# The PV matmuls of two attention units put behind one another, and one exponential moved a quarter back

## The chip, the cores and the metric
The kernel runs on one core of a Trainium2 chip. The metric is the device time of one execution in microseconds. Before the change the median of three runs is 512.85 us (512.27 to 514.27).

## The reference
A block of a conditioned transformer on 32 sequences of 128 tokens, with 128 features, 16 heads of 8 features, and a hidden width of 512. Cut to what matters:

```python
x = rmsnorm(tokens, attn_norm_w)
scale, shift = jnp.split(modulation @ film_w.T + film_b, 2, axis=-1)
x = x * (1.0 + 0.1 * jnp.tanh(scale))[:, None, :] + shift[:, None, :]
q, k, v = jnp.split(x @ qkv_w.T + qkv_b, 3, axis=-1)          # q and k then get RoPE
tokens = tokens + merge_heads(masked_attn(q, k, v, valid)) @ out_w.T + out_b
query, src = rmsnorm(tokens, sq_norm_w), rmsnorm(seq_tokens, s_norm_w)
update = merge_heads(masked_attn(query @ wq.T, src @ wk.T, src @ wv.T, svalid)) @ mha_out_w.T  # + biases
gate = jax.nn.sigmoid(jnp.concatenate([tokens, update], axis=-1) @ gate_w.T + gate_b)
tokens = tokens + gate * update
g, val = jnp.split(rmsnorm(tokens, ffn_norm_w) @ gu_w.T + gu_b, 2, axis=-1)
return tokens + jax.nn.silu(g) * val @ down_w.T + down_b

def masked_attn(q, k, v, valid_keys):
    scores = jnp.einsum('bhqd,bhkd->bhqk', q, k) / math.sqrt(HD)
    scores = jnp.where(valid_keys[:, None, None, :], scores, jnp.finfo(scores.dtype).min)
    return jnp.einsum('bhqk,bhkd->bhqd', jax.nn.softmax(scores, axis=-1), v)
```

## The kernel before
The 32 sequences are eight groups of four. Each group has a self and a cross attention, so there are 16 phases. A phase has four units, one per sequence, with all 16 heads: 64 units. Two units are a pair (32 pairs), and a pair's results leave PSUM together.

All engines run the same loop over time steps t. `n, q = divmod(t, 4)` gives a unit n and a quarter q, four heads. What an engine does in a step is written into its loop by hand, in a fixed order; it runs its list in order and is held only by semaphores. In the steps of unit n:

- TensorE makes the scores from which the maxima of unit n + 4 are taken (`max_scores`, line 366, into the two banks `ps_a` by turns), and the transposed scores of unit n (`prob_scores`, line 386, into the two banks `ps_b` by turns). q and k are split in three bf16 parts each and stacked, so both are bf16 matmuls. The scores of quarter q wait until the bank's user of two quarters ago is done.
- VectorE takes the maxima (`maxima`, line 1087) and splits them in two bf16 parts (`split_tops`). TensorE turns them (`turn_tops`, line 374), ScalarE copies them (`keep_top`, line 888), and ScalarE's DMA queue writes them as two more rows of the stacked q (`top_rows`, line 895). The scores of line 386 thus have the maxima subtracted. The first quarter of an even unit waits for that DMA (`top_in`).
- ScalarE takes the exponential of each quarter (`exps`, line 902) into `probs`, which holds an even and an odd unit. The first exponential of unit n waits until the PV matmuls of unit n - 2 are done.
- TensorE multiplies the probabilities with the values (`weigh`, line 403): per unit 16 fp32 matmuls, 32 columns of the array each, which the trace shows as 32. They write one half of the bank `ps_o`, the even unit the left, the odd one the right. The padded values hold a column of ones, so the sum of the exponentials comes along. `weigh(n - 1)` stands ahead of everything else in quarter 2 of unit n.
- VectorE takes the pair (`take_pair`, lines 1105 and 1107: transpose of `ps_o`, reciprocal of the sums) in quarter 3 of the even unit behind it, and divides it (`divide_pair`, lines 1117 and 1125) in quarter 1 of the odd one.

The other products stand between these at steps of their own: projections and value products of later groups (lines 320, 331, 353), the two output projections (`out_product` of line 415, "mo" of line 320), norms (`column_means` of line 425, for which ScalarE squares in line 931; `turn_factors` of line 433), the gate (439, 440) and the hidden layer (320, 444, 455, 461). They use three banks `ps_g` by turns, and the score banks once these are free at the end. A phase's first scores wait for the stacks of q and k (line 658, SyncE's DMA queue) and its mask row.

Of the kernel before, what the change touches and what calls it, by code (L numbers as in the profile page):

```python
# [37 lines left out]
UNITS = PHASES * NG  # L38
PAIRS = UNITS // 2
# [70 lines left out]
def build(nc, x, side, cond, mask, anw, qkv_w, qkv_b, out_w, out_b, film_w, film_b, sqw, snw, in_w, in_b,  # L110
          mo_w, mo_b, gate_w, gate_b, fnw, gu_w, gu_b, down_w, down_b, cos_t, sin_t, ident_t, out):
    with ExitStack() as ctx:
# [189 lines left out]
        def _(pe):  # L302
# [87 lines left out]
            def weigh(n):  # L390
                p, b = divmod(n, NG)
                u = n % 2
                if b == 0:
                    taken(pe, ("v", p))
                if u == 0:
                    wait(pe, o_taken, n // 2)
                pe.wait_ge(exp_done, NQ * (n + 1))
                for r in range(2):
                    for j in range(2):
                        for c in range(4):  # L400
                            h = 4 * c + 2 * r + j
                            at = 26 * h - 8 * j
                            mm = pe.matmul(  # L403
                                ps_o[32 * c:32 * c + 32, u * 256:(u + 1) * 256].rearrange(
                                    "p (b r q) -> p r b q", r=2, q=32)[:, r],
                                v_pad[p % 2][:, b, at:at + 32],
                                probs[:, u, h * S:(h + 1) * S].rearrange("k (b q) -> k b q", q=32),
                                start=(j == 0), stop=(j == 1))
                mm.then_inc(pv_done, 1)
# [82 lines left out]

            for t in range(FIRST, LAST):
                n, q = divmod(t, 4)
                if q == 2 and 0 <= n - 1 < UNITS:
                    weigh(n - 1)
                if n + LEAD == 0 and q == 0:
                    pe.wait_ge(ones_in, 16 * 2 * SETS)
# [309 lines left out]
        def _(act):  # L808
# [153 lines left out]
            for t in range(FIRST, LAST):  # L962
                n, q = divmod(t, 4)
                for m in range(PAIRS):
                    if t == top_time(m) + 1:
                        keep_top(m)
                if 0 <= n < UNITS:
                    exps(n, q)
                for m in range(PAIRS):
                    if t == top_time(m) + 1:  # L970
                        top_rows(m)
                for g in range(G):
                    sp_at, cp_at = POS[SELF, g], POS[CROSS, g]
                    for b in range(NG):
                        if g and t == s_prep(g) - 16 + x_square_at(g)[b]:
                            square(SELF, g, b)
                        if t == ck_prep(g) - 16 + (5, 6, 7, 8)[b]:
                            square(CROSS, g, b)
                        if t == s_prep(g) + 2 + b // 2:
                            keep_xm(g, b)  # L980
                    if t == s_prep(g) + 10:
                        act.wait_ge(summed[0], g + 1)
                        keep_hi(0, sp_at)
                    if t == s_prep(g) + 12:
                        act.wait_ge(summed[1], g + 1)
                        keep_hi(1, sp_at)
                    if t == s_prep(g) + 13:
                        keep_mid(0, sp_at)
                    if t == s_prep(g) + 14:
                        keep_mid(1, sp_at)  # L990
                    if t == c_prep(g) - 3:
                        residual1(g)
                    if t == c_prep(g) - 2:
                        square2(g)
                    if t == ck_prep(g) + 1:
                        keep_side(g)
                    if t == ck_prep(g) + 5:
                        keep_full(("ck", g), 1, C_CKB, cp_at)
                    if t == ck_prep(g) + 6:
                        taken(act, ("ck", g))  # L1000
                        keep_hi(1, cp_at)
                    if t == cq_prep(g) + 9:
                        keep_full(("cq", g), 0, C_CQB, cp_at)
                    if t == ck_prep(g) + 9:
                        keep_mid(1, cp_at)
                    if t == cq_prep(g) + 10:
                        taken(act, ("cq", g))
                        keep_hi(0, cp_at)
                    if t == cq_prep(g) + 13:
                        keep_mid(0, cp_at)  # L1010
                    if t == post(g, "tanh"):
                        gate(g)
                    if t == post(g, "square"):
                        square3(g)
                    for j in range(4):
                        if t == mlp(g)[0][j] + 1:
                            gated_unit(g, j)
                if t == s_prep(0) + 8:
                    keep_weights(2, four(ps_a[0])[:, 0:2, :], W_V, W_V + 2)
                    keep_late_weights("cv_weights", W_CV, W_CV + 1)  # L1020
                for o in (1, 2):
                    for p in range(2):
                        if t == s_prep(p) + (0, 14, 16)[o]:
                            stack_k(o, p)
                for k in range(4):
                    if t == (0, 3, 5, 8)[k] + 1:
                        keep_late_weights(("weights", k), (W_MO, W_GU, W_GU + 4, W_DOWN)[k],
                                          (W_MO + 3, W_GU + 4, W_GU + 8, W_DOWN + 4)[k])
                if t == 10:
                    src = full_in(act, "late")  # L1030
                    act.activation(late[:, 0:N_L], src[:, 0:N_L], ACT.Copy).then_inc(taken_sem("late"), 1)
                    taken(act, "late")
                if t == 16:
                    act.wait_ge(halves_set, 2)

        @block.vector
        def _(dve):
# [198 lines left out]
            for t in range(FIRST, LAST):  # L1236
                n, q = divmod(t, 4)
                if n % 2 == 0 and q == 0 and 0 <= (n + 2) // 2 < PAIRS:
                    split_tops((n + 2) // 2)
                if 0 <= n + LEAD < UNITS:  # L1240
                    maxima(n + LEAD, q)
                if n % 2 == 0 and q == 3 and 0 <= (n - 2) // 2 < PAIRS:
                    take_pair((n - 2) // 2)
                if n % 2 == 1 and q == 1 and 0 <= (n - 3) // 2 < PAIRS:
                    divide_pair((n - 3) // 2)
                for p in range(PHASES):
                    if t == v_time(p) + 1:
                        keep_v(p)
                for g in range(G):
                    if g and t == s_prep(g) - 16 + (14 if g < 4 else 11):  # L1250
                        means_x(g)
                    if t == ck_prep(g) - 16 + 9:
                        means_side(g)
                    if 0 < g < 4 and t == s_prep(g):
                        norm_x(g)
                    for r in range(2):
                        for which in range(2):
                            if t == s_prep(g) + 6 + 2 * r + (which if g >= 4 else 0):
                                rope(r, g, which)
                    if t == c_prep(g):  # L1260
                        mean_of(("ss2", g), ms2)
                    if t == c_prep(g) + 4:
                        normed2(g)
                    if t == post(g, "update"):
                        update(g)
                    if g >= 5 and t == post(g, "residual"):
                        residual2(g)
                    if t == post(g, "mean"):
                        mean_of(("ss3", g), ms3)
                    if t == post(g, "normed"):  # L1270
                        normed3(g)
                    for j in range(4):
                        if t == mlp(g)[2][j]:
                            hidden(g, j)
                    if t == mlp(g)[3][1] + 1:
                        add_down_bias(g)
                if t == s_prep(0) + 10:
                    order_heads(2, ps_a[0][:, 2 * D:4 * D], W_CQ)
                    dve.wait_ge(v_bias_in, 32)
                if t == 12:  # L1280
                    taken(dve, "late")
                    dve.tensor_scalar(half_gate_b[:, :], late[:, L_GB:L_GB + 1], 0.5, None, ALU.mult
                                      ).then_inc(halves_set, 1)
                    dve.tensor_scalar(half_g_b[:, :], late[:, L_GUB:L_GUB + 4], 0.5, None, ALU.mult
                                      ).then_inc(halves_set, 1)
# [45 lines left out]
```

## Time and profile before

| | |
|---|---|
| runs: median (lowest to highest) | 512.85 us (512.27 to 514.27) |
| profiled execution | 517.94 us, of which the span is 516.1 |
| mean granted TensorE clock | 0.937 of full speed |
| TensorE matmul / weight load busy | 442.1 us (86%) / 308.3 us (60%) |
| VectorE busy | 350.1 us (68%) |
| ScalarE busy | 290.4 us (56%) |
| GpSimd busy | 190.8 us (37%) |
| line 403 (PV), matmuls / weight loads | 73.3 us / 55.3 us, 2048 each |
| line 366 and line 386 (scores), matmuls | 105.0 us and 102.0 us, 1024 each |
| line 1087 (maxima) | 169.6 us, 256 of 680 ns |
| line 902 (exponentials) | 151.3 us, 256 of 595 ns |

The profiled execution is one of its own, with its own time beside its span. Busy shares are means over stages with different limits. A matmul's end is modelled, so a start minus the start before it says more than its length. "Idle before" a row is the engine's own idle time, with what released it.

### The profile page before, as it was taken

The numbers are of one execution on the slowest core, as the hardware profiler recorded it, in microseconds if no ns is written. First come the engines' busy times: TensorE is split into PE (matmuls) and PEld (weight loads), VectorE is DVE, ScalarE is ACT, GpSimd is POOL, SyncE is SP. The second block draws the span as 40 slices with busy tenths as digits, with TensorE's granted clock in tenths as the row PEclk, the third lists the DMA queues.
The fourth block names the chain that finished last, engine by engine and source line by source line (L and its number), as shares of the span: only waits on it lengthen the run. The fifth ranks groups of instructions, "written<-read, shape, count | busy, mean of one in ns | idle before, by whom it ended". The sixth has DMA issues, their size and how long they took to land.

```text
span 516.1 us, 13226 instructions
## 1 busy us (share of the span) xinstructions
PE 442.1 (86%) x5219; PEld 308.3 (60%) x5219; DVE 350.1 (68%) x655; ACT 290.4 (56%) x644; POOL 190.8 (37%) x184
## 2 busy tenths in 40 slices
PE   3546889878897986999989988999999969999897
PEld 2115375756675664666577655866586748565664
DVE  2326655878885896698677866767748856856565
ACT  4321364577566664777576648486636744556243
POOL 4451140614433163528381828254542542000010
PEclk9975778899997999799999999999989999999999
DMA  3355442354353445344443443425140320000001
GB/s 77 87 174 174 131 122 88 100 162 151 100 162 107 140 121 153 103 128 121 131 137 108 117 140 97 153 67 163 43 149 25 98 92 3 23 3 22 22 1 42
DMA packets 62942, 52.04 MB, mean 101 GB/s; under 512 B 3803, under 2 KB 61728, under 8 KB 62880
## 3 DMA queue, kind: packets, MB, share of 16 engines
q1 hardware_dynamic: 60050, 49.07, 32.2%
q10 hardware_dynamic: 2830, 2.12, 1.4%
q8 instruction: 42, 0.69, 0.6%
q14 instruction: 20, 0.16, 0.1%
HBM read 8.55 MB, written 2.11 MB: 21 GB/s over the span
## 4 chain that ended last, share of the span: by engine, by line
PE 52%; DVE 11%; DMA 10%; ACT 8%; issue 8%; SPq 5%; POOL 4%; ACTq 1%; DVEq 0%; POOLq 0%
PE ps_o L403 8%; PE ps_a L366 7%; PE ps_g L320 7%; PE ps_b L386 6%; PE ps_g L461 5%; SPq L658 4%; DMA k_st<-part_k 4%; DVE top L1087 4%; PE ps_g L444 4%; PE ps_g L353 3%; DMA q_st<-top_t 3%; ACT probs L902 2%; DMA s_in<-in_fside_BxSxS 1%; ACT turned_in L838 1%; PE ps_g L418 1%
## 5 line engine op out<-in xcount | busy, mean ns | idle before, releaser
L1087 DVE TENSOR_REDUCE top<-ps_a 128x4 f32<-128x512 f32 x256 | 169.6, 680 | 106.1 <-PE ps_a L366 104.8
L902 ACT ACTIVATE probs<-ps_b 128x512 f32<-128x512 f32 x256 | 151.3, 595 | 143.6 <-PE ps_b L386 139.5
L366 PE MATMUL ps_a<-k_st,q_st 73*128 73x128 bf16 x1024 | 105.0, 228 | 27.8 <-DMA k_st<-part_k 15.0
L366 PEld LDWEIGHTS ps_a<-k_st,q_st 73*128 73x128 bf16 x1024 | 69.8, 101 | 79.5 <-issue 59.9
L386 PE MATMUL ps_b<-q_st,k_st 75*128 75x128 bf16 x1024 | 102.0, 223 | 9.4 <-ACT probs L902 7.5
L386 PEld LDWEIGHTS ps_b<-q_st,k_st 75*128 75x128 bf16 x1024 | 69.6, 99 | 18.5 <-issue 9.2
L403 PE MATMUL ps_o<-probs,v_pad 128*32 128x128 f32 x2048 | 73.3, 287 | 0.0
L403 PEld LDWEIGHTS ps_o<-probs,v_pad 128*32 128x32 f32 x2048 | 55.3, 115 | 24.1 <-issue 14.7
L728 POOL TENSOR_TENSOR f<-f 128x4 f32<-128x4 f32 x16 | 16.6, 1038 | 98.8 <-DVE f L1136 98.8
L320 PE MATMUL ps_g<-norm,w_t 128*128 128x512 f32 x66 | 37.1, 647 | 1.2 <-DVE hid L1178 1.2
L320 PE MATMUL ps_g<-turned_in,w_t 128*128 128x512 f32 x48 | 30.3, 717 | 5.0 <-ACT turned_in L838 4.8
L444 PE MATMUL ps_g<-norm,w_t 128*128 128x512 f32 x56 | 30.1, 620 | 3.3 <-DVE quotient L1132 2.6
L461 PE MATMUL ps_g<-w_t,hid 128*128 128x128 f32 x224 | 27.4, 276 | 0.0
L765 POOL TENSOR_SCALAR unit_th<-unit_th 128x512 f32<-128x512 f32 x16 | 9.9, 620 | 45.0 <-ACT unit_th L922 45.0
L461 PEld LDWEIGHTS ps_g<-w_t,hid 128*128 128x128 f32 x224 | 26.0, 192 | 0.0
L922 ACT ACTIVATE unit_th<-ps_g,half_g_b 128x512 f32<-128x512 f32 x22 | 15.1, 686 | 14.3 <-PE ps_g L444 14.3
L1105 DVE STREAM_TRANSPOSE turned<-ps_o 128x512 f32<-128x512 f32 x32 | 22.6, 706 | 0.3 <-PE ps_o L403 0.3
L749 POOL TENSOR_TENSOR part_k<-full_k,part_k 128x512 bf16<-128x512 f32 x14 | 16.2, 1158 | 17.8 <-ACT part_k L876 17.7
L353 PE MATMUL ps_g<-w_t,turned_in 128*128 128x128 f32 x128 | 21.9, 325 | 0.2 <-ACT top_t L888 0.2
L718 POOL TENSOR_TENSOR f<-f 128x4 f32<-128x4 f32 x16 | 16.4, 1024 | 14.5 <-DVE f L1043 13.9
L744 POOL TENSOR_TENSOR full_k<-full_k,part_k 128x512 f32<-128x512 f32 x14 | 16.4, 1168 | 13.3 <-ACT part_k L872 13.3
L768 POOL TENSOR_TENSOR hid<-hid,unit_th 128x512 f32<-128x512 f32 x16 | 20.3, 1268 | 1.3
(197 smaller groups left out, 677.6 us busy)
## 6 DMA issues: line engine op xcount, KB each, us to landing
q_st<-part_q SPq DMA_DIRECT2D x126, 128.0 KB
k_st<-part_k SPq DMA_DIRECT2D x120, 128.0 KB
x_in<-in_x SPq DMA_DIRECT2D x16, 256.0 KB, 4.5
q_st<-hid SPq DMA_DIRECT2D x18, 128.0 KB
s_in<-in_fside_BxSxS SPq DMA_DIRECT2D x8, 256.0 KB, 5.7
out<-t SPq DMA_DIRECT2D x8, 256.0 KB, 2.3
k_st<-hid SPq DMA_DIRECT2D x12, 128.0 KB
swap_q<-part_q SPq DMA_DIRECT2D x8, 128.0 KB, 2.3
```

The costliest lines, as they stand in the source:

```text
L320: pe.matmul(to[:, :], w, rhs, start=True, stop=True).then_inc(done, 1)
L353: mm = pe.matmul(to[:, b * D:(b + 1) * D], src[:, b * S:(b + 1) * S], w, start=True, stop=True)
L366: mm = pe.matmul(ps_a[q % 2][:, j * S:(j + 1) * S], st[0][i][0:R_MAX, h, b * S:(b + 1) * S], st[1][i][0:R_MAX, h, b * S:(b + 1) * S], star ...
L386: mm = pe.matmul(ps_b[q % 2][:, j * S:(j + 1) * S], st[1][i][0:R_END, h, b * S:(b + 1) * S], st[0][i][0:R_END, h, b * S:(b + 1) * S], star ...
L403: mm = pe.matmul(ps_o[32 * c:32 * c + 32, u * 256:(u + 1) * 256].rearrange("p (b r q) -> p r b q", r=2, q=32)[:, r], v_pad[p % 2][:, b, at ...
L444: pe.matmul(to[:, :], w_t[:, W_GU + j, :], norm3[:, :], start=True, stop=True).then_inc(done, 1)
L461: mm = pe.matmul(to[:, b * D:(b + 1) * D], hid[:, j, b * S:(b + 1) * S], w_t[:, W_DOWN + j, :], start=False, stop=j == 3 and b == NG - 1)
L658: sp.dma_start(st[r][p % SETS][product:R_MASK:PRODUCTS, :, :], parts(r, p)[:, o, :]).then_inc(stacked[r][p % 2], 16)
L768: pool.tensor_tensor(hid[:, j, :], hid[:, j, :], unit_th[:, :], ALU.mult).then_inc(g_mul, 1)
L902: act.activation(probs[:, n % 2, q * T:(q + 1) * T], ps_b[q % 2][:, :], ACT.Exp, scale=SCALE).then_inc(exp_done, 1)
L1087: dve.tensor_reduce(top[:, n // 2 % 2, n % 2, QH * q:QH * (q + 1)], ps_a[q % 2][:, :].rearrange("p (h k) -> p h k", h=QH), AX.X, ALU.max). ...
L1105: dve.transpose(turned[:, :], ps_o[:, :]).then_inc(o_taken, 1)
```

## The change
TensorE no longer runs `weigh(n - 1)` in quarter 2 of every unit. In quarter 1 of each even unit it runs `weigh(n - 2)` and `weigh(n - 1)`, one behind the other: the even unit's comes three quarters later, the odd unit's one quarter earlier. The first exponential of an even unit would wait for the even unit's `weigh` of the pair before, so on ScalarE it moves from quarter 0 to quarter 1, ahead of that quarter's own. On VectorE `take_pair` moves from quarter 3 to 2, and `divide_pair` from quarter 1 to 0. No instruction is added or removed, and no wait is changed.

```diff
@@ TensorE
             for t in range(FIRST, LAST):
                 n, q = divmod(t, 4)
-                if q == 2 and 0 <= n - 1 < UNITS:
+                if n % 2 == 0 and q == 1 and 0 <= n - 2 < UNITS:
+                    weigh(n - 2)
                     weigh(n - 1)
@@ ScalarE
-                if 0 <= n < UNITS:
+                if 0 <= n < UNITS and (n % 2 == 1 or q > 0):
+                    if n % 2 == 0 and q == 1:
+                        exps(n, 0)
                     exps(n, q)
@@ VectorE
-                if n % 2 == 0 and q == 3 and 0 <= (n - 2) // 2 < PAIRS:
+                if n % 2 == 0 and q == 2 and 0 <= (n - 2) // 2 < PAIRS:
                     take_pair((n - 2) // 2)
-                if n % 2 == 1 and q == 1 and 0 <= (n - 3) // 2 < PAIRS:
+                if n % 2 == 1 and q == 0 and 0 <= (n - 3) // 2 < PAIRS:
                     divide_pair((n - 3) // 2)
```

TensorE's list before, from quarter 1 of unit 43 to quarter 1 of unit 44 (`ps_a` are scores for maxima, `ps_b` scores for exponentials, line 403 the PV matmuls):

```order
L366 MATMUL ps_a1<-k_st2,q_st2 128x128 x4
L386 MATMUL ps_b1<-q_st1,k_st1 128x128 x4
L403 MATMUL ps_o<-probs,v_pad0 32x4x32 x16
L366 MATMUL ps_a0<-k_st2,q_st2 128x128 x4
L386 MATMUL ps_b0<-q_st1,k_st1 128x128 x4
L366 MATMUL ps_a1<-k_st2,q_st2 128x128 x4
L386 MATMUL ps_b1<-q_st1,k_st1 128x128 x4
L366 MATMUL ps_a0<-k_st0,q_st0 128x128 x4
L386 MATMUL ps_b0<-q_st2,k_st2 128x128 x4
L320 MATMUL ps_g2<-norm3,w_t 128x512
L320 MATMUL ps_g0<-norm2,w_t 128x512
L366 MATMUL ps_a1<-k_st0,q_st0 128x128 x4
```

The same piece after (line numbers are unchanged up to 495 here):

```order
L366 MATMUL ps_a1<-k_st2,q_st2 128x128 x4
L386 MATMUL ps_b1<-q_st1,k_st1 128x128 x4
L366 MATMUL ps_a0<-k_st2,q_st2 128x128 x4
L386 MATMUL ps_b0<-q_st1,k_st1 128x128 x4
L366 MATMUL ps_a1<-k_st2,q_st2 128x128 x4
L386 MATMUL ps_b1<-q_st1,k_st1 128x128 x4
L366 MATMUL ps_a0<-k_st0,q_st0 128x128 x4
L386 MATMUL ps_b0<-q_st2,k_st2 128x128 x4
L320 MATMUL ps_g2<-norm3,w_t 128x512
L320 MATMUL ps_g0<-norm2,w_t 128x512
L403 MATMUL ps_o<-probs,v_pad0 32x4x32 x32
L366 MATMUL ps_a1<-k_st0,q_st0 128x128 x4
```

The 16 PV matmuls of unit 42 went from quarter 2 of unit 43 behind the products of unit 44's quarter 0, and those of unit 43 came up to them, so that 32 stand in one row.

ScalarE's list before, quarters 3 of unit 39 to 1 of unit 40 (line 922 and 924 are a hidden unit's tanh and copy, 907 the gate, 872 a part of k):

```order
L907 ACTIVATE gate_th<-ps_g,half_gate_b 128x512
L872 ACTIVATE part_k<-full_k 128x512
L902 ACTIVATE probs<-ps_b 128x512 x2
L922 ACTIVATE unit_th<-ps_g,half_g_b 128x512
L924 ACTIVATE hid<-ps_g,late 128x512
L902 ACTIVATE probs<-ps_b 128x512
```

And after, where each line number is one higher:

```order
L908 ACTIVATE gate_th<-ps_g,half_gate_b 128x512
L873 ACTIVATE part_k<-full_k 128x512
L903 ACTIVATE probs<-ps_b 128x512
L923 ACTIVATE unit_th<-ps_g,half_g_b 128x512
L925 ACTIVATE hid<-ps_g,late 128x512
L903 ACTIVATE probs<-ps_b 128x512 x2
```

The exponential of unit 40's quarter 0 went from ahead of the hidden unit to behind it, next to that of quarter 1.

VectorE's list before, units 10 and 11 (1087 are maxima, 1105 and 1107 take the pair, 1117 and 1125 divide it):

```order
L1087 TENSOR_REDUCE top<-ps_a0 128x4
L1087 TENSOR_REDUCE top<-ps_a1 128x4
L1105 STREAM_TRANSPOSE turned<-ps_o 128x512
L1107 RECIPROCAL inverse<-turned 128x32
L1087 TENSOR_REDUCE top<-ps_a0 128x4
L1087 TENSOR_REDUCE top<-ps_a1 128x4
L1117 TENSOR_TENSOR quotient<-turned,inverse 128x256
L1125 STREAM_TRANSPOSE att_s2<-quotient 128x256
```

And after, where each line number is three higher:

```order
L1090 TENSOR_REDUCE top<-ps_a0 128x4
L1108 STREAM_TRANSPOSE turned<-ps_o 128x512
L1110 RECIPROCAL inverse<-turned 128x32
L1090 TENSOR_REDUCE top<-ps_a1 128x4
L1090 TENSOR_REDUCE top<-ps_a0 128x4
L1120 TENSOR_TENSOR quotient<-turned,inverse 128x256
L1128 STREAM_TRANSPOSE att_s2<-quotient 128x256
```

The pair is taken one maximum earlier and divided one maximum earlier. VectorE's list at the end of the program, before (1132 and 1136 are a mean, 1185 adds the bias to a group's result):

```order
L1136 TENSOR_SCALAR f8<-quotient 128x4
L1185 TENSOR_TENSOR t2_1<-ps_g2,down_bias 128x512
L1105 STREAM_TRANSPOSE turned<-ps_o 128x512
L1107 RECIPROCAL inverse<-turned 128x32
L1117 TENSOR_TENSOR quotient<-turned,inverse 128x256
L1125 STREAM_TRANSPOSE att_c<-quotient 128x256
```

And after:

```order
L1139 TENSOR_SCALAR f8<-quotient 128x4
L1108 STREAM_TRANSPOSE turned<-ps_o 128x512
L1110 RECIPROCAL inverse<-turned 128x32
L1188 TENSOR_TENSOR t2_1<-ps_g2,down_bias 128x512
L1120 TENSOR_TENSOR quotient<-turned,inverse 128x256
L1128 STREAM_TRANSPOSE att_c<-quotient 128x256
```

The pair is taken ahead of the bias addition, and divided behind it as before.

## Rows read from the trace of the kernel before

**Rows 1.** Waits: who waited for whom: us in all, times, longest.
```profile
PE ps_a L366 <- DMA k_st<-part_k: 15.0, 3, 7.9
...
PE ps_a L366 <- DVE top L1087: 7.7, 15, 1.6
PE ps_b L386 <- ACT probs L902: 7.5, 16, 0.9
```

**Rows 2.** Busy time in two stretches: PE, PEld, DVE, ACT, POOL, clock, DMA.
```profile
333.27:345.80 12.53, 11.64 (x144) 7.42 (x142) 9.48 (x19) 9.65 (x25) 5.03 (x5) 1.00 0.16 46
120.33:129.99 9.66, 8.53 (x138) 6.03 (x137) 8.87 (x18) 6.77 (x15) 3.77 (x4) 1.00 0.57 174
```

**Rows 3.** Timeline, weight loads: start, us, name, [idle before <-releaser].
```profile
258.04 0.27 PEld L386 LDWEIGHTS ps_b<-q_st,k_st 75*128 75x128 bf16 x4
258.41 0.81 PEld L403 LDWEIGHTS ps_o<-probs,v_pad 128*32 128x32 f32 x32
259.42 0.23 PEld L366 LDWEIGHTS ps_a<-k_st,q_st 73*128 73x128 bf16 x4 [0.20 <-issue]
```

**Rows 4.** Timeline, TensorE, units 43 and 44.
```profile
336.04 1.08 PE L403 MATMUL ps_o<-probs,v_pad 128*32 128x128 f32 x32
337.05 0.40 PE L366 MATMUL ps_a<-k_st,q_st 73*128 73x128 bf16 x4
337.29 0.39 PE L386 MATMUL ps_b<-q_st,k_st 75*128 75x128 bf16 x4
...
339.40 0.38 PE L386 MATMUL ps_b<-q_st,k_st 75*128 75x128 bf16 x4 [0.69 <-ACT probs L902]
```

**Rows 5.** Timeline, ScalarE, the same stretch.
```profile
336.15 0.60 ACT L902 ACTIVATE probs<-ps_b 128x512 f32<-128x512 f32 x1 [1.63 <-PE ps_b L386]
...
338.64 0.61 ACT L902 ACTIVATE probs<-ps_b 128x512 f32<-128x512 f32 x1
```

**Rows 6.** Chain that ended last, in order of time: start, us, what.
```profile
119.79 3.46 DMA q_st<-top_t
...
166.41 4.03 DMA q_st<-top_t
...
198.91 7.68 DMA k_st<-part_k
```

**Rows 7.** Timeline, TensorE, start of the phase at unit 24.
```profile
206.84 0.58 PE L366 MATMUL ps_a<-k_st,q_st 73*128 73x128 bf16 x4 [4.39 <-DMA k_st<-part_k]
```

**Rows 8.** Timeline, ScalarE, unit 6.
```profile
103.80 0.60 ACT L902 ACTIVATE probs<-ps_b 128x512 f32<-128x512 f32 x1 [1.78 <-PE ps_b L386]
...
105.91 0.71 ACT L931 ACTIVATE norm<-ps_g,late 128x512 f32<-128x512 f32 x1
```

**Rows 9.** Timeline, VectorE, unit 10.
```profile
126.17 1.29 DVE L1087 TENSOR_REDUCE top<-ps_a 128x4 f32<-128x512 f32 x2 [0.35 <-PE ps_a L366]
127.37 0.71 DVE L1105 STREAM_TRANSPOSE turned<-ps_o 128x512 f32<-128x512 f32 x1
128.12 0.35 DVE L1107 RECIPROCAL inverse<-turned 128x32 f32<-128x32 f32 x1
```

**Rows 10.** Timeline, TensorE, two waits behind a W's new place.
```profile
138.49 0.40 PE L366 MATMUL ps_a<-k_st,q_st 73*128 73x128 bf16 x4 [1.61 <-DVE top L1087]
...
298.53 1.13 PE L444 MATMUL ps_g<-norm,w_t 128*128 128x512 f32 x2 [1.48 <-DVE quotient L1132]
```

**Rows 11.** Timeline, all engines, behind the last unit.
```profile
483.45 1.08 PE L403 MATMUL ps_o<-probs,v_pad 128*32 128x128 f32 x32
483.56 0.69 DVE L1185 TENSOR_TENSOR t<-ps_g,down_bias 128x512 f32<-128x512 f32 x1 [1.88 <-PE ps_g L461]
...
485.74 0.43 DVE L1117 TENSOR_TENSOR quotient<-turned,inverse 128x256 f32<-128x256 f32 x1
486.20 0.45 DVE L1125 STREAM_TRANSPOSE att_c<-quotient 128x256 f32<-128x256 f32 x1
...
486.69 1.13 PE L320 MATMUL ps_g<-att_c,w_t 128*128 128x512 f32 x2 [1.58 <-DVE att_c L1125]
```

## The prediction
> **What bounds the kernel now.** I read the list of waits first, then the busy time by stretches, then the order of time around single units. The waits [rows 1] say that TensorE is held by others for few microseconds: 7.7 us by VectorE in 15 waits, 7.5 us by ScalarE in 16, 15.0 us by the DMAs of the k stack in 3. So TensorE sets the pace, but never by much. In a late stretch (two units from 333.27 to 345.80) it is busy 11.64 of 12.53 us, with ScalarE at 9.65; in an early one (120.33 to 129.99) VectorE, at 8.87 of 9.66, is above TensorE's 8.53 [rows 2]. The other engines run just behind, through score banks that hold two quarters each.
>
> I call the odd unit before a merge o, the even unit e, a quarter (e,1), and the PV matmuls of one unit W. Before, one W stands ahead of (o,2) and one ahead of (e,2). After, both stand ahead of (e,1).
>
> **The change part by part.** *The switch.* W's weight loads take 0.81 us; TensorE's loads pause 0.10 us before it (258.04 + 0.27 to 258.41) and 0.20 us after it [rows 3]. So a W costs 1.11 us; two in a row 0.10 + 0.81 + 0.03 + 0.81 + 0.20 = 1.95, where 0.03 is the pace inside W (0.81/32). Saved: 0.27 a pair, 32 x 0.27 = 8.6 us. What stands between two Ws is not shown in this trace: it can be the 0.03 of a matmul, or at the other end a full pause of 0.30, and then nothing is saved. I take 0.03, since all 32 loads inside W come without a pause.
>
> The Trainium skill (TensorEngine Tiling (Array Packing), Key Properties) says that a change of the tiling mode drains TensorE, while a change of tile alone does not. The pauses of [rows 3] agree. By that rule alone the whole 8.6 us would be won, which is the first rival below.
>
> *The lead that is lost.* The saving is not where the Ws go. From (o,2) to (e,0) TensorE now comes 1.11 us early; ahead of (e,1) it pays 1.95, and at (e,2) it stands at -1.11 + 1.95 - 1.11 = -0.27. The lead of 1.11 is kept only if nothing else holds TensorE in those quarters. If another engine or DMA sets the time there, and does not itself start from the missing W, the lead turns into a wait, and the pair ends at +0.84. Unit 43 shows it: W at 336.04, scores at 337.05 and 337.29, then a wait of 0.69 us for ScalarE at 339.40 [rows 4]. ScalarE runs without idle time from the exponential at 336.15 to that at 338.64, over a hidden unit and a copy of the keys [rows 5]; it does not start earlier when W goes. I went over all 31 crossings in this way, adding the missing 1.11 us to the idle time of ScalarE and VectorE before their (o,2) work:
> - The exponents' top rows must land before the scores of (e,0). Their DMA is issued in (o,0) and takes 3.46 us to the matmul that waits for it (119.79), 4.03 at 166.41 [rows 6]. Four crossings (e = 8, 10, 18, 26) have under about 1 us to spare.
> - At three starts of a phase (e = 16, 24, 56) TensorE waits for the stack: 4.39 us at 206.84 [rows 7], behind a DMA issued at 198.91 [rows 6].
> - At seven (e = 22, 30, 38, 40, 44, 46, 52) ScalarE is behind as in unit 43, at one (e = 60) VectorE.
> - At two (e = 6, 50) the squares for a norm come late: ScalarE works from the exponential of (e,1) at 103.80 to the square at 105.91 without idle time [rows 8], and that exponential comes 0.84 us later, whatever W does.
>
> That is 17 x 1.11 = 18.9 us. At five more a part is lost, because VectorE or ScalarE had 0.3 to 0.7 us too little idle time: 2.4 us by the same count, of which I take half, 1.2, since two fall into waits already counted.
>
> *The pair taken earlier.* VectorE's transpose and reciprocal (0.71 + 0.35 us) now stand ahead of the maxima of (e,3), and the quotient and its transpose ahead of those of (o,1). In [rows 9] the maxima came in a row until 127.46 and the pair was taken behind them. TensorE's (o,1) scores wait for the maxima of (e,3). At eight crossings they had under 1.06 us to spare, which counts 1.75 us; half of it, 0.9, lies under ScalarE waits that stay. Its ends are 0 and 1.75.
>
> *The exponential held back.* The exponential of (e,0) starts when the first W ends, about 1.0 us into the pair of Ws, takes 0.60 [rows 5], and is needed by the scores of (e,2). Those come 1.7 us after the first W (0.84 and 0.20 for the second W, and three groups of scores at some 0.23, [rows 4]). The second W and the scores of (e,1) hide it, so I cost it at nothing; without that cover it would be 0.60 us a pair.
>
> *What the merged Ws hide.* They delay TensorE by 0.84 us at (e,1) and after. Where TensorE waited there, the wait shrinks: 1.48 us for VectorE's quotient at 298.53, 1.61 for a maximum at 138.49 [rows 10], and others of 0.34 to 1.4 us. With each wait cut at what its own releaser gains, I count 1.1 (e = 2), 1.85 (e = 4, 12, 20), 1.1 (30 and 46), 1.6 (38), 0.95 (40), 0.7 (36), 0.2 (42): 7.5 us. Two of the +0.84 before a stack wait vanish in it, 1.7 us.
>
> *The end.* The last W of before runs at 483.45, behind all the down products, and TensorE then waits 1.58 us for att_c at 486.69 [rows 11]. After, the Ws stand between the two halves of the down products, so the result is there 1.8 us earlier. But VectorE's bias addition (0.69 us from 483.56), which waits for the second half, is now ahead of the quotient. So the division cannot start before about 484.3 + 0.7, and att_c is done some 0.7 us earlier, not 1.8: 0.27 of it is counted, 0.4 is new.
>
> **Sum:** -8.6 + 18.9 + 1.2 + 0.9 - 7.5 - 1.7 - 0.4 = +2.8 us. The profiled execution took 517.94 us (span 516.1 and 1.84 around it); it would become 520.7. It is 1.0% above the median of the runs, 512.85; on that I put the same +2.8: **515.6 us**.
>
> The Trainium skill (Perfetto Trace Analysis, Optimizing Tensor Performance, Matmuls) says that matmul groups should rotate through PSUM banks so that the evacuation of one lies beside the next. Two Ws in a row fill one bank for 1.95 us while the score banks run dry, so that rule speaks against this change; [rows 2] show how little slack VectorE has for it early on.
>
> **Rivals.** *The switch saving stands* (faster). If ScalarE and VectorE follow TensorE's lead, because their own queue starts from its matmuls, hardly any lead is lost. For it: ScalarE and VectorE together held it for 15.2 us only [rows 1]. Against it: units such as 43. Time: with no lead lost and nothing hidden, -8.6, or 504.3; with half of the 17 lost, +2.8 - 9.4 = -6.6, or 506.3.
>
> *The two cancel.* If 3 of the 17 crossings keep their lead, -3.3 makes it -0.5: 512.4. For it: what lies under 0.3 us of slack is read from one execution. The forecast is nearer to this than to any other.
>
> *The held exponential blocks ScalarE* (much slower). It is in order, so all behind it waits for the first W as well. The price is up to 0.60 us where ScalarE has no idle time left by (e,2); at the eight or so crossings where it paces TensorE that adds 4.8: 520.4. Against it: the other work of (e,0) now goes ahead of the exponential and uses the time. It decides when the scores of (e,2) wait for ScalarE after most merges.
>
> *The change does not do what it says* if a wait falls between the two Ws, for the exponential of (o,3). But the scores of (e,1) waited for that same exponential before, and now a whole W stands ahead of the second one. I give that no chance of its own.
>
> **How the numbers follow.** Forecast 0.42, cancel 0.24, saving stands 0.22, exponential blocks 0.12. The forecast's own range is 512.5 to 519. The range of 8 in 10 reaches halfway into the saving and to the blocked exponential: 508.5 to 520.5. A measurement of this kernel tells about 0.5% (2.6 us) from no change. Faster by more: 0.22 + 0.04 = 0.26. Within: 0.20 of cancel and 0.12 of the forecast, 0.32. Slower: 0.42.
>
> **What would show it.** The weight loads of both Ws in one run of about 1.65 us with no pause inside, 32 times: the switch. New or longer waits of TensorE in (o,2) to (e,0), for top_t's DMA at e = 10 and 18, for ScalarE at e = 44: the lost lead. The wait of 1.48 us at e = 38 gone: the cover. Scores of (o,1) waiting for maxima more often than 15 times: the earlier pair. The forecast is wrong if TensorE's waits in (o,2) to (e,0) grow by under 10 us in all.

## The result and the profile after

The changed kernel is slower: 531.53 us in the median of four runs (530.29 to 535.73), beside 512.56 us (512.15 to 514.27) for the kernel before on the same chip. The ratio is 1.0367, with a 95% interval of 1.032 to 1.0413. A repetition (e5 below), with the kernel before beside it again, gave 1.0316 (1.0258 to 1.0374). The forecast was 515.6 us: slower, but by 0.5%, and the time lies outside its range. The profiled execution took 535.73 us with a span of 533.9; before it was 517.94 and 516.1, so this pair of profiles differs by 17.8 us. In most kernels here some executions lie over 1.5% above the fastest, at a lower granted clock; the ratios leave them out, but the profiles of e2, e5, e7, e9 and e11 are of such executions.

The page of the changed kernel, with the busy time of each engine and 40 slices of the span (PEclk: granted clock of TensorE in tenths):

```profile
span 533.9 us, 13225 instructions
## 1 busy us (share of the span) xinstructions
PE 450.4 (84%) x5219; PEld 322.2 (60%) x5219; DVE 350.4 (66%) x655; ACT 289.8 (54%) x644; POOL 191.1 (36%) x184
...
PEclk9875788878987987699999999998989988989999
```

The same row of the page of before:

```profile
PEclk9975778899997999799999999999989999999999
```

TensorE does the same matmuls and is busy 8.3 us longer (442.1 before). The reason is in the last two rows: many more slices under 9, in the first half above all. The granted clock has two levels here, 2.4 and 1.2 GHz. The kernel spends 97.1 us of the span at the lower one, against 65.5 before; taken over TensorE's busy time only, half of that is lost: 43.6 us against 27.3. The difference of the profiles so divides into +16.3 us of this, +9.5 us of TensorE's idle time (80.0 against 70.5) and -8.6 us of switches, 17.2 of the 17.8 us. This is bookkeeping: what TensorE loses at half clock is not all time that the kernel loses, as the experiments show.

The waits of the changed kernel (who waited for whom: us, times, longest), to be held against [rows 1]:

```profile
DVE top L1090 <- PE ps_a L366: 122.2, 72, 6.8
...
ACT probs L903 <- PE ps_b L386: 83.2, 94, 8.2
ACT probs L903 <- PE ps_o L403: 79.1, 29, 7.2
...
PE ps_a L366 <- DVE top L1090: 16.4, 25, 1.3
...
PE ps_a L366 <- DMA k_st<-part_k: 14.6, 3, 7.6
...
PE ps_b L386 <- ACT probs L903: 7.7, 11, 1.4
...
PE ps_g L425 <- ACT norm L932: 6.5, 6, 1.7
```

TensorE waits for VectorE 25 times instead of 15, 16.4 us instead of 7.7. ScalarE waits for PV matmuls in 29 of the merges; that is the held exponential.

The weight loads of one merge (columns as in [rows 3]):

```profile
281.52 1.69 PEld L403 LDWEIGHTS ps_o<-probs,v_pad 128*32 128x32 f32 x64 [0.17 <-issue]
283.40 0.23 PEld L366 LDWEIGHTS ps_a<-k_st,q_st 73*128 73x128 bf16 x4 [0.20 <-issue]
```

64 loads in one run of 1.69 us with no pause inside, and again 0.20 behind it. There are 32 such runs, and none has a pause inside. 24 of them take 1.69 us; 8 fall wholly or in part into stretches of half clock and take up to 3.19. One switch of two is gone, as counted.

TensorE at the merge in unit 10:

```profile
120.56 0.40 PE L366 MATMUL ps_a<-k_st,q_st 73*128 73x128 bf16 x4 [1.01 <-DVE top L1090]
...
122.06 0.40 PE L386 MATMUL ps_b<-q_st,k_st 75*128 75x128 bf16 x4 [0.51 <-DMA q_st<-top_t]
122.39 3.27 PE L403 MATMUL ps_o<-probs,v_pad 128*32 128x128 f32 x64
125.59 0.61 PE L366 MATMUL ps_a<-k_st,q_st 73*128 73x128 bf16 x4
```

Two short waits, and behind them the 64 PV matmuls take 3.27 us instead of 1.96 at full clock. The next scores come 3.20 us after their start. VectorE, which fed on those scores, stands still meanwhile:

```profile
122.72 0.68 DVE L1090 TENSOR_REDUCE top<-ps_a 128x4 f32<-128x512 f32 x1
126.24 0.69 DVE L1090 TENSOR_REDUCE top<-ps_a 128x4 f32<-128x512 f32 x1 [2.83 <-PE ps_a L366]
```

The merge in unit 42 is at full clock and shows the other half. TensorE:

```profile
337.66 1.96 PE L403 MATMUL ps_o<-probs,v_pad 128*32 128x128 f32 x64
339.55 0.40 PE L366 MATMUL ps_a<-k_st,q_st 73*128 73x128 bf16 x4
...
342.07 0.27 PE L374 MATMUL ps_g<-ident_b,top_part 128*128 128x128 bf16 x2 [1.45 <-DVE norm L1152]
```

and VectorE:

```profile
339.98 0.69 DVE L1090 TENSOR_REDUCE top<-ps_a 128x4 f32<-128x512 f32 x1 [4.03 <-PE ps_a L366]
340.59 0.68 DVE L1188 TENSOR_TENSOR t<-ps_g,down_bias 128x512 f32<-128x512 f32 x1
341.19 0.74 DVE L1152 SCALAR_TENSOR_TENSOR norm<-t,late,ps_g 128x512 f32<-128x512 f32 x1
```

The bias addition and the norm stand behind the maxima of (e,1) in VectorE's list. These scores now come behind the run of PV, so VectorE idles 4.03 us although it has other work, and TensorE waits 1.45 us for that work later. Before, TensorE's wait at the same place was 0.34 us:

```profile
332.27 0.27 PE L374 MATMUL ps_g<-ident_b,top_part 128*128 128x128 bf16 x2 [0.34 <-DVE norm L1149]
```

### The profile page after: what moved, and what is told of

Same layout as the page of the kernel before. It is cut to its first block, busy times and chain, and to the rows that moved or that the text cites. A ratio compares the mean times of both kernels' runs of the same rounds, so it can differ in the third digit from the quotient of the medians.

```text
span 533.9 us, 13225 instructions
## 1 busy us (share of the span) xinstructions
PE 450.4 (84%) x5219; PEld 322.2 (60%) x5219; DVE 350.4 (66%) x655; ACT 289.8 (54%) x644; POOL 191.1 (36%) x184
## 4 chain that ended last, share of the span: by engine, by line
PE 51%; DVE 11%; ACT 10%; issue 8%; DMA 7%; SPq 5%; POOL 5%; ACTq 2%; DVEq 0%; POOLq 0%
PE ps_o L403 11%; PE ps_a L366 7%; PE ps_g L320 6%; PE ps_b L386 5%; SPq L659 5%; PE ps_g L461 5%; DMA k_st<-part_k 4%; DVE top L1090 4%; PE ps_g L444 3%; ACT probs L903 2%; PE ps_g L353 2%; DMA q_st<-top_t 1%; PE ps_g L338 1%; DMA q_st<-part_q 1%; ACT junk L829 1%
## 5 line engine op out<-in xcount | busy, mean ns | idle before, releaser
L366 PE MATMUL ps_a<-k_st,q_st 73*128 73x128 bf16 x1024 | 108.2, 233 | 36.2 <-DVE top L1090 16.4
L366 PEld LDWEIGHTS ps_a<-k_st,q_st 73*128 73x128 bf16 x1024 | 74.0, 104 | 90.5 <-issue 58.7
L386 PE MATMUL ps_b<-q_st,k_st 75*128 75x128 bf16 x1024 | 105.3, 228 | 8.8 <-ACT probs L903 7.7
L386 PEld LDWEIGHTS ps_b<-q_st,k_st 75*128 75x128 bf16 x1024 | 72.5, 102 | 18.2 <-issue 12.3
L403 PEld LDWEIGHTS ps_o<-probs,v_pad 128*32 128x32 f32 x2048 | 61.9, 122 | 14.9 <-issue 13.0
L745 POOL TENSOR_TENSOR full_k<-full_k,part_k 128x512 f32<-128x512 f32 x14 | 16.4, 1168 | 14.5 <-ACT part_k L873 14.5
L769 POOL TENSOR_TENSOR hid<-hid,unit_th 128x512 f32<-128x512 f32 x16 | 20.2, 1265 | 1.3
```

Of the source, the lines that this page charges most:

```text
L366: mm = pe.matmul(ps_a[q % 2][:, j * S:(j + 1) * S], st[0][i][0:R_MAX, h, b * S:(b + 1) * S], st[1][i][0:R_MAX, h, b * S:(b + 1) * S], star ...
L386: mm = pe.matmul(ps_b[q % 2][:, j * S:(j + 1) * S], st[1][i][0:R_END, h, b * S:(b + 1) * S], st[0][i][0:R_END, h, b * S:(b + 1) * S], star ...
L403: mm = pe.matmul(ps_o[32 * c:32 * c + 32, u * 256:(u + 1) * 256].rearrange("p (b r q) -> p r b q", r=2, q=32)[:, r], v_pad[p % 2][:, b, at ...
L769: pool.tensor_tensor(hid[:, j, :], hid[:, j, :], unit_th[:, :], ALU.mult).then_inc(g_mul, 1)
```

## The experiments

Ratios are to the kernel before, measured beside it on the same chip; a bracket holds the 95% interval. Where no ratio stands, too few runs entered for one. "Idle" is TensorE's idle time and "lost" what its busy time loses at half clock, both in the one profiled execution. "Lost" varies between executions of one kernel (30.8 and 38.7 us in e3 and e9), so a difference of a few microseconds in it decides nothing by itself.

**e1: VectorE's moves undone**

```diff
-                if n % 2 == 0 and q == 2 and 0 <= (n - 2) // 2 < PAIRS:
+                if n % 2 == 0 and q == 3 and 0 <= (n - 2) // 2 < PAIRS:
                     take_pair((n - 2) // 2)
-                if n % 2 == 1 and q == 0 and 0 <= (n - 3) // 2 < PAIRS:
+                if n % 2 == 1 and q == 1 and 0 <= (n - 3) // 2 < PAIRS:
                     divide_pair((n - 3) // 2)
```

> The changed kernel with the two VectorE moves undone: the pair is taken in quarter 3 and divided in quarter 1 again, TensorE and ScalarE as changed. By the theory that the granted clock makes most of the loss (the changed kernel spends 97 us of its span at the lower level against 65 before, 16.3 us lost by it, TensorE's idle time grew by 9.5 and the switches gave 8.6 back), these moves matter little: 530 to 532 us. If VectorE is what holds TensorE between the crossings (the waits of L366 for VectorE went from 7.7 to 16.4 us, and the stretches between the crossings are 8.4 us longer in sum), undoing them brings 4 to 8 us: 523 to 528.

Measured: 527.43 to 541.81 us, median 535.15, beside 514.09 for before; idle 76.9 us, lost 43.1. Nothing came back that these runs could show, but they spread over 14 us and can't settle the 4 to 8 us of the rival. The profile shows a small price: line 366 waits for VectorE 17 times (9.0 us) instead of 25 (16.4), and the seven pairs from unit 28 to unit 42, at full clock in both, take 96.64 us instead of 98.00. Most of the loss stays without the moves.

**e2: the held exponential alone** (before, and on ScalarE)

```diff
-                if 0 <= n < UNITS:
+                if 0 <= n < UNITS and (n % 2 == 1 or q > 0):
+                    if n % 2 == 0 and q == 1:
+                        exps(n, 0)
                     exps(n, q)
```

> The kernel before with one part of the change alone: the first exponential of an even unit waits until quarter 1; the PV matmuls and VectorE stay where they were. The prediction counted nothing for it: 512 to 514 us. The rival by which ScalarE pays for it (in the changed kernel the exponentials wait 79 us behind the PV matmuls, 29 times) has 0.60 us a pair on the path at 10 to 30 of 32 pairs: 518 to 530 us, with longer waits of L386 for ScalarE.

Measured: 1.0006 (0.9961 to 1.0052), 512.86 us. Holding it back costs nothing where the PV matmuls stay. The rival is out in this form; with the PV moved, it was not tested by itself.

**e3 and e9: the two PV groups a quarter apart** (the changed kernel, and)

```diff
+                if n % 2 == 0 and q == 0 and 0 <= n - 2 < UNITS:
+                    weigh(n - 2)
                 if n % 2 == 0 and q == 1 and 0 <= n - 2 < UNITS:
-                    weigh(n - 2)
                     weigh(n - 1)
```

> The changed kernel with the two PV groups one quarter apart: the even unit's in quarter 0, the odd unit's in quarter 1 of the next even unit. 32 runs of PV become 64 again, so 32 switches come back (+8.6 us). If it is the two groups in one run that lower the granted clock, the half-clock time falls from 97 to some 65 us and 16 us come back: 522 to 525 us. If it is only that the order uses up TensorE's lead at the crossings, nothing comes back: 536 to 541 us.

> The kernel with the two PV groups a quarter apart, again with more rounds. If the run of two costs the clock and VectorE's supply, as its first profile says (12.8 us less lost at half clock, 6.4 us less idle time of TensorE, 8.6 us of switches back), it lies 1.0 to 1.6% above the kernel before, where the changed kernel lies 3.2 to 3.7% above it. If the first rounds were chance: 3% or more.

Measured: 1.0123 (1.0001 to 1.0245), then 1.016 (1.0095 to 1.0224). It pays 32 more switches than the changed kernel and is still some 8 us faster. Its profiles have 73.6 and 73.4 us of idle time and 30.8 and 38.7 lost. From unit 28 to unit 42, at full clock, it is not faster (98.98 and 98.95 us beside 98.00), so its gain lies elsewhere.

**e4 and e6: waits filled, on the changed kernel.** Before 23 of the waits in the first 220 us TensorE does matmuls whose result nobody reads. The place in unit 10 gets 7 of them:

```diff
+            def fill(k):
+                if not k:
+                    return
+                wait(pe, o_taken, weighed[0])
+                for _ in range(k):
+                    pe.matmul(ps_o[:, 256:384], ident[:, :].bitcast(BF16)[:, 0:128],
+                              ident[:, :].bitcast(BF16)[:, 0:128], start=True, stop=True)
...
                 if 0 <= n + LEAD < UNITS:
                     max_scores(n + LEAD, q)
+                fill(FILL.get((n, q, 'b'), 0))
                 if 0 <= n < UNITS:
                     prob_scores(n, q)
```

> The changed kernel, and in 23 of the waits of its first 220 us TensorE does matmuls whose result nobody reads (128x128 bf16, as many as fill some 90% of each wait, into a half of ps_o that is free then). The work that counts and all waits stay. If the granted clock makes the loss and falls because TensorE stood still, the windows at half clock in that stretch (76 us before the fills) mostly go: the time falls by 15 to 30 us, to 502 to 516. If the waits themselves are the loss and the clock only goes along, the time stays within 2 us of 531.5, or rises by the fills that outlast their wait (up to 5 us).

> The changed kernel once more, as the measure for the other runs beside it: 530 to 533 us by every theory.

> The changed kernel with 23 waits of its first 220 us filled, again. Its one profiled execution had a span of 521.2 us (clock 0.961), three others 529.5 (0.942 to 0.955), so the first three rounds do not decide. If the granted clock is the loss: 519 to 524 us, 8 to 12 below the changed kernel beside it. If it is not: within 3 us of it.

Measured: e4 522.97 to 531.68 us, none of it in the 502 to 516 that it should have reached if the clock made the loss. e6, the same kernel with more runs: 524.79 us, 1.0175 (1.0098 to 1.0252), beside 1.0316 for the changed kernel itself (e5, a plain repetition). So 0.0141 x 512 = 7.2 us came back, by the two intervals 2 to 12, just under the 8 to 12 expected. The stretch up to the scores of unit 28, where nearly all fills lie, in one row each: length, busy PE, PEld, DVE, ACT, POOL, clock. First the changed kernel, then e4, then e5 and e6, the same two kernels again:

```profile
0.00:236.63 236.63, 184.77 (x2124) 132.98 (x2124) 150.56 (x291) 124.16 (x305) 87.33 (x86) 0.83 0.41 123
```

```profile
0.00:226.27 226.27, 190.60 (x2597) 142.41 (x2597) 150.46 (x291) 124.06 (x305) 87.16 (x86) 0.95 0.44 129
```

```profile
0.00:233.79 233.79, 182.40 (x2124) 131.74 (x2124) 151.50 (x291) 124.33 (x305) 87.37 (x86) 0.85 0.42 125
```

```profile
0.00:228.08 228.08, 192.89 (x2597) 144.10 (x2597) 150.16 (x291) 124.23 (x305) 87.23 (x86) 0.94 0.43 128
```

The work that counts is the same, 473 matmuls more are done, and the stretch is 10.4 us shorter in the first pair of profiles, 5.7 in the second. The clock is 0.95 and 0.94 instead of 0.83 and 0.85. The merge in unit 10 in e4:

```profile
117.97 0.56 PE L500 MATMUL ps_o<-ident 128*128 128x128 bf16 x7
118.36 0.39 PE L386 MATMUL ps_b<-q_st,k_st 75*128 75x128 bf16 x4
118.68 1.95 PE L403 MATMUL ps_o<-probs,v_pad 128*32 128x128 f32 x64
```

The wait is full of work, and the same 64 PV matmuls take 1.95 us, not 3.27. Later, where nothing was filled and the clock is full in both, the pairs of the two kernels have the same length to 0.01 us (pairs 15 to 20).

**e7: waits filled, on the kernel before** (19 waits, the same function)

> The kernel before with 19 of its waits in the first 220 us filled in the same way. It loses 27.3 us in busy time at half clock, 22 of it there. If that time is on the path: 500 to 507 us. If VectorE or ScalarE takes its place there: 510 to 514.

Measured: 1.001 (0.9951 to 1.0069). The low clock left some places and came at others: lost fell only from 27.3 to 22.8 us, and the fills gave nothing. Not every microsecond at half clock is on the path either: ahead of unit 0 the clock stood at half for 20.5 us instead of 27.3, and its first scores came only 0.5 us earlier (60.47 for 61.01).

**e10: the maxima's scores between the two groups** (the changed kernel, and)

```diff
                 if n % 2 == 0 and q == 1 and 0 <= n - 2 < UNITS:
                     weigh(n - 2)
-                    weigh(n - 1)
...
                 if 0 <= n + LEAD < UNITS:
                     max_scores(n + LEAD, q)
+                if n % 2 == 0 and q == 1 and 0 <= n - 2 < UNITS:
+                    weigh(n - 1)
                 if 0 <= n < UNITS:
                     prob_scores(n, q)
```

> The changed kernel with one group moved: the scores for the maxima of the even unit's quarter 1 stand between the two PV groups instead of behind them. 32 switches come back (+8.6 us), VectorE gets these scores 0.95 us earlier. If the undivided run of 1.9 us is what starves VectorE (the wait of 1.45 us for it at L374 in pair 21 and those like it) and lowers the clock: 520 to 527 us. If the late place of the even unit's PV alone is the loss: 536 to 540 us, the changed kernel plus the switches.

Measured: 1.0355 (1.0277 to 1.0432), the same as the changed kernel and between the two expectations. 8.6 us of switches were paid and about as much came back (7.3 of it as less lost, 36.3). Alone it decides nothing.

**e12: merged only from unit 28 on**

> The change only from the crossing ahead of unit 28 on; the first half as before. If the halves stand for themselves, the second half is 10.6 us longer in the changed kernel's profile, 6.6 us of it in pairs 14 to 30 by the shortest time that each pair took in any run of either order (so at full clock): 519 to 524 us, 1.3 to 2.2% above before. If the loss starts with the low clock and the late DMAs of the first half and only goes on from there: 512 to 516 us.

Measured: 1.0239 (1.0164 to 1.0315), a little above the first expectation. The second half alone carries about two thirds of the loss. Pairs 21 to 26 took 87.92 us here, 88.08 in the changed kernel, 81.68 before. The loss at half clock in the profile is 27.1 us, as before (27.3), and the mean granted clock of the runs that enter the ratio is 0.929 beside 0.936: most of this half's loss comes without the clock.

**e13 and e14: the run of two kept, scores first.** e13 puts the scores for the maxima of (e,1) ahead of it, e14 those for the exponentials too (shown):

```diff
-                if n % 2 == 0 and q == 1 and 0 <= n - 2 < UNITS:
-                    weigh(n - 2)
-                    weigh(n - 1)
...
                 if 0 <= n + LEAD < UNITS:
                     max_scores(n + LEAD, q)
                 if 0 <= n < UNITS:
                     prob_scores(n, q)
+                if n % 2 == 0 and q == 1 and 0 <= n - 2 < UNITS:
+                    weigh(n - 2)
+                    weigh(n - 1)
```

> The changed kernel with the run of two PV groups behind the scores for the maxima of the even unit's quarter 1, ahead of those for its exponentials. No switch comes back. If VectorE's missing supply makes the waits (1.45 us at L374 in pair 21, 1.21 us at L366 in pair 17): 3 to 7 us below the changed kernel, 2.0 to 2.8% above before. If the place behind the crossing is the loss: within 2 us of the changed kernel, 3.0 to 3.8% above before.

> As before it, with both score groups of quarter 1 ahead of the run of two. ScalarE still waits for the even unit's PV with its held exponential, and gets it 0.46 us later. If the supply of both engines makes the waits: 1.5 to 2.5% above before. If the place behind the crossing is the loss: 3.0 to 3.8%. If the held exponential becomes the bound now: above 3.8%.

Measured: e13 1.0322 (1.026 to 1.0385), idle 74.8 us, lost 47.5. e14 1.0223 (1.0151 to 1.0296), idle 74.3, lost 36.0. The merge in unit 42 in e14, TensorE and then VectorE:

```profile
327.60 0.39 PE L386 MATMUL ps_b<-q_st,k_st 75*128 75x128 bf16 x4
327.92 1.96 PE L403 MATMUL ps_o<-probs,v_pad 128*32 128x128 f32 x64
...
330.27 0.28 PE L374 MATMUL ps_g<-ident_b,top_part 128*128 128x128 bf16 x2
```

```profile
327.80 0.69 DVE L1090 TENSOR_REDUCE top<-ps_a 128x4 f32<-128x512 f32 x1 [2.04 <-PE ps_a L366]
328.41 0.68 DVE L1188 TENSOR_TENSOR t<-ps_g,down_bias 128x512 f32<-128x512 f32 x1
329.01 0.74 DVE L1152 SCALAR_TENSOR_TENSOR norm<-t,late,ps_g 128x512 f32<-128x512 f32 x1
```

Bias and norm now run beside the PV matmuls, and the wait of 1.45 us is gone. From the scores of unit 28 to those of unit 42, at full clock in all three, the rows of before, of the changed kernel and of e14:

```profile
229.41:326.82 97.41, 90.01 (x1150) 63.43 (x1147) 73.14 (x138) 63.35 (x142) 55.01 (x52) 1.00 0.43 124
```

```profile
236.63:334.63 98.00, 88.78 (x1149) 64.07 (x1148) 73.15 (x138) 63.99 (x144) 55.82 (x53) 1.00 0.41 120
```

```profile
229.45:324.44 94.99, 88.25 (x1147) 64.75 (x1147) 73.05 (x137) 63.52 (x144) 56.04 (x53) 1.00 0.42 125
```

With the same merges, only two groups of scores moved, these seven pairs take 3.0 us less than in the changed kernel and 2.4 less than before. The changed order repeats there: 98.06 us in e4, 98.02 in e12. In e13 the wait of 1.45 us is gone too, and the idle time fell by 5.2 us, but the loss at half clock was 3.9 us more, and no time was won. By what was written before the run, e13 speaks against the supply of VectorE as the whole cause, and e14 for the supply of both engines.

**e8, e11, e15, e16: merges at some crossings only**

```diff
+MERGED = (2, 4, 12, 22, 28, 36, 38, 40, 62, 64)
...
-                if q == 2 and 0 <= n - 1 < UNITS:
+                if n in MERGED and q == 1:
+                    weigh(n - 2)
+                    weigh(n - 1)
+                if q == 2 and 0 <= n - 1 < UNITS and n + n % 2 not in MERGED:
                     weigh(n - 1)
```

The exponential and the pair's moves follow the same list. These are crossings that got shorter in the changed kernel, chosen from its profile.

> The PV groups of a pair in one run only at ten of the 32 crossings (ahead of units 2, 4, 12, 22, 28, 36, 38, 40, 62 and behind 63), with the held exponential and the VectorE moves only there; elsewhere as before. These are the crossings that got shorter in the changed kernel without a change of the clock (0.3 to 2.4 us each). If each crossing stands for itself: 507 to 510 us, 3 to 5 below the kernel before. If a gain at one crossing is given back at the next, or the clock falls elsewhere: 512 to 518.

> As the selected merges, without those ahead of units 22, 28 and 36, which gave nothing there: over the two pairs around each, the profile of that kernel is +0.2, +0.6 and +0.2 us against before. If the gain is the sum of the crossings: 1 us below it, 1.2 to 1.5% below the kernel before. If it comes from a clock that happens to be higher: anything between 0.5 and 1.2% below.

> The merges ahead of units 2, 4, 12, 38, 40, 62 and behind 63, each with the scores for the maxima ahead of the run. If the supply of VectorE counts: 0.5 to 1 us below the same merges without it, 1.0 to 1.4% below before. If not: 0.7 to 1.1% below.

> The ten selected merges again, beside the others of this call: 0.8 to 1.5% below the kernel before.

Measured: e8 0.9886 (0.9845 to 0.9927), 507.75 us; e16, the same kernel again, 0.9885 (0.98 to 0.9969); e11 with seven merges 0.9909 (0.9862 to 0.9955); e15, these seven with the scores first, 0.9899 (0.9854 to 0.9944). All four beat the kernel before, by about 1%, and cannot be told from one another. In e8's profile the span is 9.1 us shorter than before; 2.7 us of switches, 1.0 of idle time and 6.6 of less lost (20.7) would make 10.3. So a good part of the gain may be the clock, and which crossing gives what is not shown.

## Why the prediction was wrong

**The switch (-8.6).** Right for the loads: 32 runs with no pause inside, 1.69 us at full clock. The pauses around them were read in one place: behind a run it is 0.20 us 29 times and 0.38 three times, ahead of it 0.10 to 0.20 us 19 times and 0.76 eight times. From unit 28 to unit 42 TensorE's busy time fell by 1.2 us (90.01 to 88.78), where 7 x 0.27 = 1.9 was counted.

**The lead (+18.9 and +1.2) and what the merges hide (-7.5 and -1.7).** The sign was right, both sizes were too large. From the scores of (o,1) to those of (e,0) TensorE's idle time grew from 20.2 to 31.1 us, over all 31 crossings: +10.9, where 18.4 was counted (20.1, less the 1.7). That is just above the bound of 10 that I had set. In the rest of the loop, where waits should have shrunk by 7.5, it went from 21.4 to 21.0 only. Single places came as worked out: the wait of 1.48 us at e = 38 [rows 10] is gone, and from the scores of (o,1) to those of (e,2) that crossing took 0.88 us less (-0.27 + 1.11 - 1.6 = -0.76 counted); e = 44 [rows 4] took 0.87 more (0.84), with a wait of 1.35 us for ScalarE. But the merges also made new waits, such as the 1.45 us in unit 42. I had looked at the engines' idle time ahead of (o,2), not at what stands behind the scores of (e,1) in VectorE's list. e14 shows this for the waits that it removes: there the PV stands later still, so the supply made them, not the late place of the PV. So one step that failed is what the merges hide: -7.5 counted, -0.4 measured. The two errors nearly cancel by luck, and the sum of idle time, +9.5, is close to the +11.4 that the prediction held (2.8 + 8.6).

**The granted clock, not in the sum.** This is the other step that failed, a term put at nothing without a reason: durations were taken from rows at full clock, and the sum was made as if TensorE's work cost the same afterwards. In the profiles TensorE's work lost 16.3 us more at half clock. The runs support some of it: the filled waits (e6) gave back 7.2 us with the same order and the same PV runs. More was not shown. e7 says that such time is not always on the path, and 16.3 us is what TensorE's work lost, not what the kernel did. An estimate from the mean granted clocks says the same. Within one kernel, over all runs without fills that enter the ratios, 0.01 more of the clock goes with some 3.2 us less time. In e5 the changed kernel ran at 0.921 and 529.6 us on average, the kernel before beside it at 0.941 and 512.3: by that slope some 6 us of the 17.4 go with the clock.

The second half is longer even without it: over the 15 pairs from unit 28 on (pairs 14 to 27 and 29), by the shortest time each took in any profile of either order (before, e2 and e7; the changed kernel, e4 to e6), it is 5.5 us, most of it in pairs 21, 22 and 25. The prediction's own terms give these pairs only +1.4 (15 switches -4.1, nine lost leads +10.0, hidden -4.6). So the clock is not the whole miss, and the rest of it, beyond these pairs, is not resolved.

The Trainium skill (TensorE: Matmul & The Clock Gate, A second HAM failure mode: psum-queue depth-cycling) describes a kernel in which TensorE idles briefly between groups of matmuls often enough that its clock swings between the two levels. The rows of unit 10 and of e4 agree: after waits of 1.01 and 0.51 us the PV matmuls took 3.27 us, and with these waits filled 1.95. I had not weighed that rule.

**The earlier pair (+0.9).** L366 waited for VectorE 25 times instead of 15, at (o,1) 6 times with 4.7 us where there was no such wait. In e1, with the moves undone, these six waits are gone, and seven pairs at full clock took 1.4 us less. The term was right in kind; for the whole kernel its price is not resolved.

**The held exponential (0).** Right alone (e2); line 386 waited for ScalarE 7.7 us in the changed kernel and 7.5 before. The 79.1 us that ScalarE waits for PV matmuls in the changed kernel are idle time of an engine that is not the bound.

**The end (-0.4).** TensorE's wait for att_c is 1.16 us, before 1.58 [rows 11]: as counted.

**The rivals.** "The saving stands" and "the two cancel" fell. None named the clock, though the row of the clock stood on the page with 65.5 us at half clock, and the changed kernel gave the same work in longer lumps with more waits between.

**What stays open.** Whether the run of two PV groups itself, or only the waits around it, brings the clock down. Taking the groups apart lowered the loss (e3: 30.8 us, e9: 38.7), and so did e14 with the run whole (36.0), but e13 raised it (47.5). These are single profiles. Executions of one kernel differ by several microseconds here, since a stretch of half clock falls on one pair or another: pair 22 took 15.83 us in the changed kernel and 18.76 in e4, where 3.02 of it were lost.

## What to carry over

Where TensorE waits often and briefly, a reordering can change its clock. So look at the granted clock beside each wait that the change adds, and give a forecast a term for it; filling some waits with idle matmuls is a cheap test (it brought 7.2 us here in one kernel and nothing in the other). Before two groups are merged, look at what stands behind the first scores that now come late, in every engine's list, and put the work that feeds the others ahead of the long run (e14: 3.0 us in seven pairs). And a merge that gains at one crossing and loses at another need not be made everywhere: ten of 32 were worth 1.1% here.

## What was unexpected of the hardware

- The same 64 PV matmuls took 3.27 us in one place and 1.95 in the same place once 7 matmuls had filled the 0.51 us before them (and others the waits before that): the granted clock had fallen after waits of 1.0 and 0.5 us.
- 473 matmuls added to TensorE, the engine that sets the pace, made the first stretch 10.4 and 5.7 us shorter in two pairs of profiles.
- At full clock six pairs of the changed kernel and of e4 agree to 0.01 us. That is not always so: in e5, the changed kernel again, pairs 15 and 19 took 0.6 and 0.7 us more at full clock. Mostly what differs between executions is where the half clock falls, 1.5 to 1.7 us at a time in a pair that TensorE paces.
